# One image pair's 56-point transforms as four 64x64 matmuls instead of one block-diagonal one, and a new place for the row transform

## The reference

```
h = layer_norm(x, n1_g, n1_b)
xf = rfft2(h, axes=(1, 2), norm='ortho')          # 56 x 29 frequencies, 64 channels
o1 = relu(xf * w1 + b1)                           # complex, block diagonal: 8 blocks of 8 channels
o2 = softshrink(o1 * w2 + b2, 0.01)               # complex, block diagonal
h = irfft2(o2) + h + x
out = gelu(layer_norm(h, n2_g, n2_b) @ mw1 + mb1) @ mw2 + mb2 + h
```

## Time and profile before

| | before |
|---|---|
| median of three runs | 806.96 us |
| the profiled execution, and its span from the first to the last instruction | 809.76 us, 808.0 us |
| TensorE matmul busy | 765.6 us (95%) |
| VectorE busy | 561.5 us (69%) |
| ScalarE busy | 393.7 us (49%) |
| POOL busy | 263.1 us (33%) |
| mean granted TensorE clock | 0.984 |

### The profile page before, as it was taken

One profiled execution on the slowest core, in us unless ns is written; L12 is line 12 of the kernel. 1 busy time (PEld: TensorE's weight loads), 2 busy tenths in 40 slices (PEclk: granted clock), 3 DMA queues, 4 the chain that ended last, 5 costly groups with the idle time before them and its releaser, 6 DMA issues.

```text
span 808.0 us, 18673 instructions
## 1 busy us (share of the span) xinstructions
PE 765.6 (95%) x7561; PEld 531.2 (66%) x7561; DVE 561.5 (69%) x1860; ACT 393.7 (49%) x757; POOL 263.1 (33%) x107
## 2 busy tenths in 40 slices
PE   7998998998999999999999999999999999989887
PEld 5994558886666676657765777486748665747333
DVE  4568988799777677767685858585958695733651
ACT  0011006743756374736563656475646544755365
POOL 5000000953740364035412551245223622362000
PEclk9899999999999999999999999999999999999999
DMA  9934002011000210112010300130000000000012
GB/s 273 277 97 144 3 2 81 1 48 35 1 25 24 74 41 14 35 46 70 13 35 24 92 13 24 35 92 13 24 30 18 12 25 24 24 12 24 24 35 69
DMA packets 10375, 39.50 MB, mean 49 GB/s; under 512 B 1282, under 2 KB 1410, under 8 KB 8834
## 3 DMA queue, kind: packets, MB, share of 16 engines
q1 hardware_dynamic: 10290, 38.31, 16.4%
HBM read 25.46 MB, written 12.85 MB: 47 GB/s over the span
## 4 chain that ended last, share of the span: by engine, by line
PE 84%; DVE 12%; issue 2%; ACT 1%; DMA 0%; DVEq 0%; ACTq 0%
PE psum L1115 11%; PE psum L1124 11%; PE psum L1020 7%; PE psum L1061 7%; PE psum L1030 6%; PE psum L1072 6%; PE psum L1045 6%; PE psum L1093 5%; PE psum L1005 4%; PE psum L844 4%; PE psum L895 3%; PE psum L1133 3%; PE psum L990 3%; DVE stats L587 2%; PE psum L1106 2%
## 5 line engine op out<-in xcount | busy, mean ns | idle before, releaser
L1314 ACT ACTIVATE hid<-psum,hbias 128x448 f32<-128x448 f32 x224 | 123.8, 635 | 80.6 <-PE psum L1115 80.6
L411 POOL TENSOR_TENSOR rbuf<-ybuf,prm 112x2560 f32<-112x2560 f32 (+2 forms) x7 | 31.8, 4539 | 224.8 <-DVE hbuf L816 130.4
L1115 PE MATMUL psum<-n2T,mw1s 64*128 64x448 f32 x448 | 102.7, 576 | 1.7 <-ACT n2T L1307 1.7
L429 POOL TENSOR_TENSOR p_y<-layer,clamped 128x512 f32<-128x512 f32 x64 | 75.6, 1181 | 80.1 <-DVE clamped L697 80.1
L1124 PE MATMUL psum<-hid,prm 128*64 128x448 f32 x448 | 96.3, 552 | 1.9 <-DVE oslice L706 1.9
L691 DVE TENSOR_TENSOR layer<-psum,prm 128x512 f32<-128x512 f32 x64 | 40.3, 630 | 42.8 <-PE psum L1061 42.8
L1061 PEld LDWEIGHTS psum<-w2s,o_g 128*64 128x64 f32 x1856 | 60.1, 138 | 14.4 <-issue 8.9
L416 POOL TENSOR_TENSOR hbuf<-hbuf,prm 112x3584 f32<-112x3584 f32 x8 | 49.6, 6204 | 59.9 <-DVE n L632 59.9
L1072 PEld LDWEIGHTS psum<-cst,p_y 128*128 128x128 f32 x512 | 61.2, 192 | 10.6 <-issue 6.3
L1072 PE MATMUL psum<-cst,p_y 128*128 128x112 f32 x512 | 66.8, 277 | 0.5 <-DVE layer L691 0.5
L1061 PE MATMUL psum<-w2s,o_g 128*64 128x64 f32 x1856 | 66.1, 224 | 0.9 <-ACT o_g L1292 0.6
(11 more groups left out here) (135 smaller groups left out, 1382.3 us busy)
## 6 DMA issues: line engine op xcount, KB each, us to landing
xin<-x_dram SPq DMA_DIRECT2D x8, 1568.0 KB, 8.3
out_dram<-oslice SPq DMA_DIRECT2D x56, 224.0 KB, 2.2
ybuf<-x_dram SPq DMA_DIRECT2D x2, 1568.0 KB, 15.9
fbuf<-x_dram SPq DMA_DIRECT2D x2, 1568.0 KB, 19.1
xin<-x_dram SPq DMA_DIRECT2D x4, 392.0 KB, 4.9
n<-x_dram SPq DMA_DIRECT2D x1, 1568.0 KB, 21.3
n<-x_dram SPq DMA_DIRECT2D x4, 392.0 KB, 13.2
prm<-params_dram SPq DMA_DIRECT2D x1, 742.0 KB, 4.2
```

The lines of the kernel that those rows point to most:

```text
L411: nc.gpsimd.tensor_tensor(r3, y3, row("b1", ws.stop - ws.start), ALU.add).then_inc(r_begun, 1)
L429: nc.gpsimd.tensor_tensor(yk, a, b, ALU.subtract).then_inc(y_ready, 1)
L1115: nc.tensor.matmul(t[:, 0:4 * ROWS], mw1s[C * v:C * v + C, HH * m:HH * m + HH], n2T[C * v:C * v + C, s % 2, :], start=True, stop=True).the ...
L1314: nc.scalar.activation(hid[:, s % 2, m, v, :], bank[CH_MLP[i].bank[k]][:, 0:4 * ROWS], ACT.Gelu, bias=hbias[:, m:m + 1]).then_inc(c_act, 1)
```

## The change

- The row transform is cut into quarters q of 8 channel pairs. Each former matmul becomes four, one for each image b and column half h, of 56 rows x 56 weights x 58 columns, which use the four 64x64 parts of the array. For that the second image moves to partition 64: working buffers have 128 partitions (`RP = 128`), `xT`, `mlp_t` and the inverse transform's matrix are padded, and `f1`, `f2` are half as wide.
- The column transform is cut the same way (channel half h, image b), 56 rows x 64 weights x 58 columns. ScalarE takes each bank with one operation (the first two also need a single-element one, with a wait each).
- `dft_h(i + 1, q)` moves from the head of step i+1 to the tail of step i, between `inv_h` and the last MLP pieces. `inv_w`'s result goes to `o_g` instead of `u_r`, so that `u_r` is free for it. `mlp_out(i-2, 6)` now stands before the column transform and `turn_out(i-2, 6)` after its second quarter.
- Results of `inv_h` rotate over three banks instead of two (pairs 1 to 6), `whiten` over three instead of mostly one; two `whiten` banks move from before the wait shown above to behind it.
- ScalarE takes five banks of `layer_1`, VectorE three. VectorE's `multiply_rstd` for the second half and its first whitened banks come after its share of `layer_1`.
- POOL's gain is cut into four, `begin_residual` into three and `add_h` into four operations; `add_h` waits for the first half of `multiply_rstd` only. SP stores each slice with two DMAs, and loads x later in its order.

```
-L1_DVE = (1, 3, 5, 7)
+L1_DVE = (3, 5, 7)
+    return (1, 2, BANK_X)[k % 3] if 0 < i < PAIRS - 1 else B_BANK[FIN + k]
...
+                    for j in range(8):
+                        for b in range(2):
+                            for h in range(2):
+                                one = nc.tensor.matmul(t[b][C * h:C * h + H, j * KR:(j + 1) * KR],
+                                                       h_w[C * b:C * b + H, 8 * q + j, h, :], cc("f1")[C * b:C * b + H, :],
+                                                       start=True, stop=True)
...
+                    for j in range(n):
+                        at = (8 * q + j) * 128
+                        for h in range(2):
+                            for b in range(2):
+                                one = nc.tensor.matmul(t[h][C * b:C * b + C, j * KR:(j + 1) * KR],
+                                                       u_r[C * h:C * h + H, at + C * b:at + C * b + C], cc("f2")[C * h:C * h + H, :],
+                                                       start=True, stop=True)
...
-                    dft_h(i)
+                    if i > 1:
+                        mlp_out(i - 2, SLICES - 1)
+                    dft_w(i, 0)
                     if ahead and i > 0:
                         whiten(i + 1, [0])
-                    dft_w(i)
-                    if ahead and i > 0:
-                        whiten(i + 1, [1])
-                    layer_1(i)
+                    dft_w(i, 1)
+                    if i > 1:
+                        turn_out(i - 2, SLICES - 1)
+                    dft_w(i, 2)
+                    layer_1(i, [0])
+                    dft_w(i, 3)
+                    layer_1(i, [2, 4, 6])
                     if i == 0:
                         folded_weights()
-                    if ahead and i > 0:
-                        whiten(i + 1, [2])
...
+                    mlp_in(i - 1, 5)
                     inv_h(i, 0)
+                    mlp_out(i - 1, 4)
+                    if ahead:
+                        dft_h(i + 1, 0)
+                    transpose_n(i - 1, 6)
                     inv_h(i, 1)
+                    if ahead:
+                        dft_h(i + 1, 1)
+                    turn_out(i - 1, 4)
                     inv_h(i, 2)
+                    mlp_in(i - 1, 6)
+                    mlp_out(i - 1, 5)
+                    if ahead:
+                        dft_h(i + 1, 2)
+                        inv_h(i, 3)
+                        turn_out(i - 1, 5)
+                        dft_h(i + 1, 3)
...
                 def ln2(i):
                     mean_rstd(i, 1)
-                    if i < PAIRS - 2:
-                        ev_whiten(i + 2, [0])
-                    for k in range(2):
-                        multiply_rstd(i, k)
+                    multiply_rstd(i, 0)
...
+                    if behind:
+                        multiply_rstd(i - 1, 1)
+                    whitened_next(0, 1, 2)
```

More of the change, by code:

```diff
@@ L37 @@
 ROWS = 2 * H
+RP = 128
 FREE = W * C
@@ L1004, in whiten @@
                             w = 4 * k + j
[L1005 removed]
+                            last = nc.tensor.matmul(t[:, j * 128:(j + 1) * 128], xT[:, w * RP:(w + 1) * RP],
                                                     wy[:], start=(i > 0), stop=True, skip_group_check=(i == 0))
                         last.then_inc(pe_a, 1)
[L1009 to L1022 removed]
@@ L1024, in dft_w @@
-                def dft_w(i):
-                    pe.wait_ge(b_act, i * B_ACT + b_done("act", S2 - 1))
-                    for k in range(8):
-                        t = free_b(i, S2 + k)
-                        for j in range(min(4, KF - 4 * k)):
-                            last = nc.tensor.matmul(t[:, j * 4 * KF:(j + 1) * 4 * KF], u_r[0:ROWS, (4 * k + j) * 128:(4 * k + j + 1) * 128],
-                                                    cc("f2", ROWS), start=True, stop=True)
-                        last.then_inc(pe_b, 1)
@@ L1034, in layer_1, with free_rows @@
-                def layer_1(i):
+                def free_rows(i, q):
+                    if i == 0 and q < 3:
+                        pe.wait_ge(whitened, 7 + 2 * q + 1)
+                    elif i == 1 and q < 2:
+                        pe.wait_ge(b_dve, b_done("dve", FIN + 2 * q + 3))
+                    elif i < 2:
+                        pe.wait_ge(b_act, i * B_ACT + b_done("act", S1 + 2 * (q % 2) + 1))
+                    else:
+                        pe.wait_ge(c_act, (i - 2) * C_ACT + CH_MLP[i - 2].act_done["hid", 5 + q // 2, q % 2, 1])
+                    return [bank[row_bank(i, 2 * q + b)] for b in range(2)]
@@ L1035, in layer_1 @@
+                def layer_1(i, ks):
                     if i == 0:
                         pe.wait_ge(s_masked, 6)
-                    for k in range(0, 8, 2):
+                    for k in ks:
                         part, half = k // 4, k // 2 % 2
@@ L1160, in whiten_next @@
                     def whiten_next(j):
-                        if ahead and i > 0 and j < 3:
-                            whiten(i + 1, [4 + j])
+                        if ahead and i > 0:
+                            whiten(i + 1, [3 + j])
                     def and_x(s, what):
@@ L1239, in _ @@
                 whiten(1, range(7))
+                for q in range(4):
+                    dft_h(0, q)
                 step(0, True, True, False)
@@ L1404, in _ @@
                 last.then_inc(norm1_step, 2)
+                for q in range(4):
+                    ev_dft_h(0, q)
                 step(0, True, False)
```

349 lines of the change are left out of this document (186 added, 163 removed).

## The result

| | forecast | measured |
|---|---|---|
| changed kernel | 802.0 us (788 to 814) | 820.17 us, median of four (816.82 to 821.06) |
| kernel before, on the same chip | 806.96 us | 807.09 us, median of four (805.65 to 809.62) |
| ratio | 0.994 | 1.0151, 95% interval [1.0113, 1.0189] |
| middle step, from `mlp_in(5)` to the next | 82.98 us | 84.20 and 83.14 us in turn |

The profiled execution took 819.82 us with a span of 818.0 us, 10.0 us more than before. Its mean granted clock was 0.957 against 0.984, though TensorE's own work had shrunk.

The account below looks back on a forecast made before the run. The prediction took TensorE to bound the kernel, with VectorE becoming the bound after the change. Its terms (-1.0, -1.7, +0.5, -2.8, +0.2) sum to -4.8 us, taking 806.96 to 802 us, range 788 to 814.

Parts of the forecast that it names:

- The matmuls: Row and column transforms: a quarter of 64 passes on four parts takes 1.0 us; TensorE's work falls 5.4 us a step.
- Rival 2: Passes in the quarters start only every 25 to 30 ns: about 825 or 837 us, slower; chance 0.15.
- VectorE becomes the bound: Middle step's layer_1 wait: VectorE ends at T 37.25 (us from mlp_in(5)), TensorE idles from 32.7 to 37.3.
- The clock: Behind that idle time, TensorE's clock falls in each middle step, costing 1.3 us, bounds 0 and 3.4.
- steps 2 to 6: The middle steps: each gains nothing (+0.1 us), together +0.5 us.
- Rival 3: Two clock falls in a row in each middle step, 3.0 instead of 1.3 us: about 811 us; chance 0.13.
- Pair 1: Its row transform starts at once, layer_1 bound by ScalarE, less moved whiten and wider transposes: -1.7 us.
- The beginning: Everything up to the first row matmul: no change, 0 us.
- pair 0: From first row matmul to first layer_2, row transform and column part held by ScalarE's copies: an estimate of -1.0 us.
- Step 7: Last step, no whiten moved behind the wait, its clock fall there before: -2.8 us.
- the tail: The tail and last MLP after step 7: +0.2 us.
- Rivals 2 to 4: The fourth: VectorE fills its idle time before turn_out(6), ScalarE sets the wait, no falls: about 778 us; chance 0.04.

Follow-up runs that it names:

- e1b_fill4: Changed kernel plus four filling matmuls (results unused) ahead of TensorE's wait for layer_1's readers, steps 2 to 7: 807.34 us.
- e2_order: Changed kernel with VectorE's statistics 5 to 7 placed before its last MLP slice (ev_mlp) instead of behind it: 806.72 us.
- e3_pool1: Changed kernel with POOL's order in pair 1 changed: begin_residual first, two gain quarters, a wait for the first multiply_rstd, then the rest: 814.55 us.
- e5_all: Changed kernel with VectorE's statistics before its last MLP slice, POOL's new pair 1 order, and ScalarE's table load early: 800.96 us.
- e9_fill1: e7_allfill with its two filling matmuls in step 1 as well: 790.73 us.
- e1_fill: Changed kernel plus nine filling matmuls (results unused) ahead of TensorE's wait for layer_1's readers, steps 2 to 7: 827.55 us.
- e6_full: Changed kernel with each four 64x64 matmuls of the transforms replaced by one full matmul of 116 columns: 833.82 us.
- e7_allfill: e5_all plus two filling matmuls ahead of TensorE's wait for layer_1's readers, steps 2 to 7: 791.82 us.

## Why the prediction was wrong, step by step

**The matmuls: right.** A quarter was put at 1.0 us (0.85 to 1.9) and took 1.01 and 1.09. Rival 2 did not occur. The Trainium skill's floor of about 25 ns from start to start (TensorE: Matmul & The Clock Gate, section "Wait — 56ns, not 53.3ns?") would have made it 1.6. The trace differs from it: 1.01 us for 64 passes is 16 ns a pass, so with four parts in turn that floor doesn't hold here.

**VectorE becomes the bound: right.** "It ends at T 37.25": 37.63. TensorE's idle time, 4.6 us: 4.28, released by VectorE. ScalarE's end at T 34.7: 35.4. "Without the clock a step would be 81.7": 81.72 in e1b_fill4. The transfer of a bank to ScalarE cost nothing while VectorE was late. In e2_order ScalarE's ten operations end the wait, so there it may cost; no run takes the bank back.

**The clock: the step where the middle failed.** "Fully under work it costs half of 3.4 [...] I take 1.3, bounds 0 and 3.4 (two in a row)." The falls came in each middle step as forecast, but one of 1.42 us and one of 2.48 alternate. Over steps 2 to 6 that is 3 x 2.48 + 2 x 1.42 = 10.3 us instead of 6.5, and less five times 1.16 (82.88 - 81.72) it makes +4.5, measured +4.65. Rival 3 (two in a row) had the mechanism for every other step. The argument set against it, that TensorE is fully busy right behind the wait, was no protection: the low clock begins at 467.70, before TensorE resumes at 469.28, and goes on through a stretch in which TensorE is busy 3.40 of 3.40 us.

**Pair 1: the step that failed most, 6.7 us off.** The sum had -1.7, "less the moved `whiten` and the wider transposes". The contention with POOL was weighed at one place only, `multiply_rstd` beside `add_h`, and taken at 0. There it held: the second half took 2.06 us, and POOL was the one that became longer (10.10 us for 7.97; of its four pieces the third, which starts 0.12 us behind VectorE's operation, takes 3.93 us, the others 2.11 to 2.12). "POOL's cut pieces are the same elements" is true and misses the point: the pieces hang on the quarters of `dft_h(1)`, which come earlier, so POOL's work moved onto `mean_rstd`. The earlier trace rows had the mechanism, 0.43 against 1.02 us; its price there was one POOL operation for each VectorE operation, and five tiny ones in a row make 6.5 us (9.86 - 3.32). In e3_pool1 this was worth 4.2 of the 6.7 us: 2.4 of waiting and 1.8 of the clock's fall at 215. The other 2.5 are the term itself. With POOL out of the way the stretch ahead of the wait is only 0.9 us shorter than before the change (50.45 against 51.37), and behind it 1.8 us longer (44.01 against 42.24), where two `whiten` banks had moved to. There ScalarE's `layer_1` ends a wait of 2.06 us; why the matmuls' gain comes to so little is open.

**The beginning and pair 0.** The beginning was put at no change and came to +0.95 at the first row matmul. A wait added at ScalarE's start took the table load with it: 0.54 us of the 0.95 are there at the first `whiten` (122.85 against 122.31). The other 0.41 arise between it and the row matmul, 19.17 us for 18.76, and are not the load's. In e5_all, with the load early again and the clock falling at the same places as before the change (65 and 120 us), the first `whiten` starts at 122.19, but the row matmul at 141.84, still 0.77 later than before. The cause of that part is open. Pair 0 was an estimate of -1.0 and came to +1.99, and there the clock fell for 6.8 us at 150.3. In e9_fill1 the clock held, and the same stretch (142.46 to 163.17) took 20.71 us against 21.29 before (20.68 and 20.94 in e1_fill and e3_pool1, where it held too). That is -0.58: the term had the right sign and nearly the size. The fall took 2.6. TensorE idles 1.12 us at 147 in the changed kernel as in e9_fill1; why the clock fell in one and not in the other is open.

**Step 7 and the tail: right**, -2.54 for -2.8 and -0.09 for +0.2. The fall in step 7 became one of 6.8 us, but it cost 1.76 us (75.58 against 73.82 with the clock held), what the prediction had taken one of 3.4 to cost.

The terms missed by 3.0 (pair 0), 6.7 (pair 1), 4.2 (steps 2 to 6) and 1.0 us (beginning), all to the same side. Of these 14.9 us the clock made about 8.2 (2.6, 1.8 and 3.8 in the first three) and the wait behind POOL 2.4; the rest is open or mis-sized terms. Rivals 2 to 4 were built on single steps in the middle; none had its place in the first two pairs, which cost more than the middle did.

Open: what decides between no, one and two stretches of low clock. Also whether another order of ScalarE's work would take away the last 2.6 us of the wait, which was not tried.

## What to carry to other kernels

When work is taken off the engine that sets the pace, read what the next engine does ahead of the shared wait: here three groups of statistics in front of the operation with the late input instead of behind it were worth 13 us, more than the whole change was to bring. An idle time of TensorE is paid twice where the clock falls behind it; a few matmuls without purpose in the idle time, ending before the wait does, are a cheap test of the second payment, and sometimes the remedy. And for each operation that is moved or cut on POOL, look at what VectorE runs at its new time, in the first and last rounds of a loop too, since small operations there can each wait for a whole POOL operation.

## What the runs showed of the hardware

- The clock's falls came in lengths of 3.4 and 6.8 us. With the same 4.28 us of idle time in each step the two alternated. A fall of 3.4 us cost 1.4 to 1.6 us of a step, one of 6.8 us 1.8 to 2.9 (the most in e6_full, 88.09 - 85.22). An idle time of 2.05 to 2.06 us at the same place brought a fall of 3.4 us in e7_allfill and none in e3_pool1.
- Four parts of 64x64 in turn start a pass every 16 to 17 ns on average (64 in 1.01 and 1.09 us). Full matmuls of 116 columns took 1.68 to 1.88 us for 16, 105 to 117 ns each.
- Five VectorE operations of 0.19 to 0.26 us took 1.17 to 1.85 us beside back-to-back POOL operations, each ending about 0.1 us after a POOL operation. One-input statistics beside POOL kept their pace of one every 0.127 us (56 in 7.18 us).
- ScalarE's table load (1.28 us) stands behind whatever its first operation waits for: at 0.73 us without the wait, at 47.65 with it.
